# Seven block products of V in one row ahead of both output projections, with VectorE's turns and reads in another order

## The reference

```python
q = heads(x @ Wq + bq)
k = heads(x @ Wk + bk)
v = heads(x @ Wv + bv)
scores = jnp.einsum('bhqd,bhkd->bhqk', q, k) * scale
scores = jnp.where(mask[:, None] == 0, -jnp.inf, scores)
attn = jax.nn.softmax(scores, axis=-1)
out = jnp.einsum('bhqk,bhkd->bhqd', attn, v)
out = out.transpose(0, 2, 1, 3).reshape(b, s, D_MODEL)
x = _layernorm(x + (out @ Wo + bo), axis=-1)
```

## Time and profile before

| what | before |
|---|---|
| median of three runs | 808.75 us |
| the profiled execution | 808.37 us |
| its span, first to last instruction | 806.6 us |
| TensorE busy | 799.6 us (99%) |
| VectorE busy | 635.5 us (79%) |
| GpSimd busy | 540.2 us (67%) |
| ScalarE busy | 267.5 us (33%) |
| mean granted clock of TensorE | 0.998 |

### The profile page before, as it was taken

One profiled execution on the slowest core, in us unless ns is written; L12 is line 12 of the kernel. 1 busy time (PEld: TensorE's weight loads), 2 busy tenths in 40 slices (PEclk: granted clock), 3 DMA queues, 4 the chain that ended last, 5 costly groups with the idle time before them and its releaser, 6 DMA issues.

```text
span 806.6 us, 26965 instructions
## 1 busy us (share of the span) xinstructions
PE 799.6 (99%) x11777; PEld 680.2 (84%) x11777; DVE 635.5 (79%) x1008; ACT 267.5 (33%) x349; POOL 540.2 (67%) x437
## 2 busy tenths in 40 slices
PE   9999999999999999999999999999999999999997
PEld 7888888888888888888888888888888888888876
DVE  5869777878778887778887787877878777876895
ACT  6642333322333222333223332223332333323223
POOL 0387668766678676776766767666866768755672
PEclk9999999999999999999999999999999999999999
DMA  9335435254453434534345344544525435234342
GB/s 330 127 81 173 116 113 179 84 150 130 120 177 98 147 109 119 176 114 134 117 115 171 123 132 119 156 130 119 164 81 171 125 106 178 71 108 120 94 110 103
DMA packets 65110, 106.64 MB, mean 132 GB/s; under 512 B 11744, under 2 KB 28640, under 8 KB 62944
## 3 DMA queue, kind: packets, MB, share of 16 engines
q1 hardware_dynamic: 52512, 87.85, 34.9%
q10 hardware_dynamic: 12480, 17.06, 8.2%
HBM read 54.53 MB, written 16.78 MB: 88 GB/s over the span
## 4 chain that ended last, share of the span: by engine, by line
PE 99%; DMA 0%; DVE 0%; issue 0%; POOLq 0%; POOL 0%
PE ring L373 16%; PE ring L374 15%; PE ring L375 15%; PE ring L525 7%; PE ring L526 7%; PE ring L529 7%; PE psum_s L476 6%; PE psum_s L446 6%; PE ring L467 6%; PE psum_s L480 6%; PE psum_s L478 6%; DMA x_raw<-in_xt 0%; PE ring L393 0%; PE ring L401 0%; PE ring L397 0%
## 5 line engine op out<-in xcount | busy, mean ns | idle before, releaser
L1186 POOL TENSOR_TENSOR soft<-soft,top 128x1024 f32<-128x1024 f32 x62 | 122.6, 1977 | 21.2 <-DVE top L973 21.2
L237 POOL TENSOR_TENSOR soft<-soft,inverse 128x1024 f32<-128x1024 f32 x62 | 118.8, 1917 | 26.0 <-DVE inverse L980 25.9
L977 DVE TENSOR_REDUCE total<-soft 128x16 f32<-128x1024 f32 x62 | 75.3, 1214 | 54.2 <-ACT soft L719 54.2
L719 ACT ACTIVATE soft<-soft 128x1024 f32<-128x1024 f32 x62 | 65.9, 1062 | 112.5 <-POOL soft L1186 112.5
L373 PE MATMUL ring<-x_hi,wk_hi 128*128 128x512 f32 x256 | 102.8, 401 | 0.0
L374 PE MATMUL ring<-x_lo,wk_hi 128*128 128x512 f32 x256 | 99.9, 390 | 0.0
L375 PE MATMUL ring<-x_hi,wk_lo 128*128 128x512 f32 x256 | 99.8, 390 | 0.0
L525 PE MATMUL ring<-wo_hi,ot_hi 128*128 128x512 f32 x252 | 99.2, 394 | 0.0
L526 PE MATMUL ring<-wo_lo,ot_hi 128*128 128x512 f32 x252 | 98.9, 393 | 0.0
L754 ACT CAST s_hi<-v 128x1024 fp32r<-128x1024 f32 x27 | 28.3, 1046 | 207.7 <-DVE v L909 207.7
L373 PE MATMUL ring<-x_hi,wq_hi 128*128 128x512 f32 x248 | 96.7, 390 | 0.0
(11 more groups left out here) (127 smaller groups left out, 1862.0 us busy)
## 6 DMA issues: line engine op xcount, KB each, us to landing
pt<-soft SPq DMA_DIRECT2D x248, 64.0 KB, 2.4
x_raw<-in_xt SPq DMA_DIRECT2D x15, 1024.0 KB, 6.8
row<-in_x SPq DMA_DIRECT2D x60, 256.0 KB, 2.7
out_rows<-row SPq DMA_DIRECT2D x60, 256.0 KB, 2.6
pt<-soft ACTq DMA_DIRECT2D x232, 64.0 KB, 2.4
v<-in_xt SPq DMA_DIRECT2D x27, 512.0 KB, 4.5
adj<-in_adj SPq DMA_DIRECT2D x16, 128.0 KB, 2.7
kt<-in_wk SPq DMA_DIRECT2D x4, 256.0 KB, 6.0
```

What stands on the lines that cost most here:

```text
L237: ops.tensor_tensor(soft_of(c), soft_of(c), on_keys(inverse[:, c % 2, :]), ALU.mult).then_inc(normed, 1)
L977: nc.vector.tensor_reduce(total[:, c % 2, :], by_row_head(soft_of(c)), AX_XY, ALU.add).then_inc(summed, 1)
L1186: nc.gpsimd.tensor_tensor(soft_of(c), soft_of(c), on_keys(top[:, c % 2, :]), ALU.subtract).then_inc(centred, 1)
```

## The change

On TensorE all seven products stand in a row, P3 ahead of P7, and both output projections behind them; the wait for `ot_lo_done` is now behind the seventh product. The product P3 waits for the read of P5, as the third read, which is written out as `READ_5 = 3`. On VectorE `turn(b)` stands straight behind `turn(a)`, ahead of the read of P1; P5 is read before P4; `split_ot` comes behind the read of P6; the two last reads (P3 first, then P7) come ahead of the add of the projection.

```diff
-P1, P2, P4, P5, P6, P7, P3, PARTS = 1, 2, 3, 4, 5, 6, 7, 7
+P1, P2, P4, P5, P6, P3, P7, PARTS = 1, 2, 3, 4, 5, 6, 7, 7
+
+READ_5 = 3
...
             def last_products(m):
+                pe.wait_ge(v_read, v_reads(m) + READ_5)
+                product(other_sums(), *inputs_sum(4), *weights_block(1, 1), adds=True)
                 pe.wait_ge(v_read, v_reads(m) + P6)
                 product(first_sums(), *inputs_sum(3), *weights_sum(3), adds=True)
-                product(other_sums(), *inputs_sum(4), *weights_block(1, 1), adds=True)
...
                 first_products(p)
+                last_products(p)
                 pe.wait_ge(ot_lo_done, p)
                 project_out(a - 2)
-                last_products(p)
                 project_out(b - 2)
...
-                dve.wait_ge(v_part, v_reads(m) + P4)
-                nc.vector.tensor_tensor(quarter(m, 1, 0), second(1), bias_of(0), ALU.add).then_inc(v_read, 1)
                 dve.wait_ge(v_part, v_reads(m) + P5)
                 nc.vector.tensor_tensor(quarter(m, 1, 1), other_sums(), bias_of(1), ALU.add).then_inc(v_read, 1)
+                nc.vector.tensor_tensor(quarter(m, 1, 0), second(1), bias_of(0), ALU.add).then_inc(v_read, 1)
...
+                dve.wait_ge(v_part, v_reads(m) + P3)
+                dve.wait_ge(v_read, v_reads(m) + P6)
+                nc.vector.tensor_tensor(quarter(m, 0, 1), other_sums(), quarter(m, 0, 1), ALU.add).then_inc(v_read, 1)
                 dve.wait_ge(v_part, v_reads(m) + P7)
-                dve.wait_ge(v_read, v_reads(m) + P6)
                 nc.vector.tensor_tensor(both, first_sums().unsqueeze(1).to_broadcast([P, 2, HALF]), both,
                                         ALU.add).then_inc(v_read, 1)
-                dve.wait_ge(v_part, v_reads(m) + P3)
-                nc.vector.tensor_tensor(quarter(m, 0, 1), other_sums(), quarter(m, 0, 1), ALU.add).then_inc(v_read, 1)
...
+                turn(b)
                 if p >= 1:
                     read_first(p)
+                    read_middle(p)
                     split_ot(p - 1)
-                turn(b)
-                if p >= 1:
-                    read_middle(p)
+                    read_last(p)
+                    add_y(a - 2)
+                    row_sums(a - 2)
                 else:
                     read_v(b)
-                if p >= 1:
-                    add_y(a - 2)
-                    read_last(p)
-                    row_sums(a - 2)
```

## The result

The changed kernel takes **830.95 us** (median of five runs, 829.09 to 832.6) against 808.95 us of the kernel before in the same comparison (808.1 to 809.65). The ratio is 1.027, with a 95% interval of 1.0257 to 1.0283: slower by 22 us. Its profiled execution took 831.51 us, of which the span is 829.6.

The account below looks back on a forecast made before the run. TensorE, busy 799.6 of 806.6 us, was taken to bound the kernel. A net 0.62 us a pass plus 0.30 for late passes gave 26 x 0.92 + 2.44 = 26.4 us on 808.37: 835 us, range 820 to 846.

Parts of the forecast that it names:

- forecast A: Main case: the first projection waits for VectorE's later split, also held by late normalisations; 835 us, 828 to 842, chance 0.62.
- The chain: VectorE's masks come 0.40 us later, so normalisation, turn, read 1, product 6, its read, split and projection follow; wait costs 0.68.
- B: Rival: the 0.40 is absorbed, product 6 is not held, only the split's place costs, 0.49 us a pass; 823 us, chance 0.16.
- The restart: TensorE, waiting for VectorE, starts its first matmul 0.14 us behind the end of VectorE's instruction.
- The fresh start: On TensorE after a wait, the first projection pays 0.10 us more; products take 0.70 to their last matmul instead of 0.60.
- The saved switches: On TensorE, fewer switches between products and projections save some 0.03 us each, 0.06 us a pass.
- D: Rival: not slower; the split is ready when TensorE comes and only switches count, 0.8 us saved; 807.6 us, chance 0.04.
- The late passes: GpSimd's waits for the row's load make tile b's normalisation late in some passes; 0.30 us a pass on average.
- C: Rival: row loads land 0.65 us late in all passes, each costing 1.27 us; 844 us, chance 0.14.
- The first pass: Outlier: its normalisation ends 3.12 us behind its first product, so the change costs 2.44 us there.
- What would show it: Signs: gap of 0.5 to 1.3 us before each first projection, smaller one before product 6, period about 25.7 us.
- VectorE's hand-over: VectorE's next instruction starts before the last one ends; otherwise turn to read and read to split each take 0.08 us longer.

Follow-up runs that it names:

- e1: TensorE's row of seven products with both projections behind it, put alone into the kernel before, VectorE's order unchanged: 858.31 us, ratio 1.0614.
- e3: The changed kernel with the turn of tile b moved behind the split of the mixed heads: 820.28 us, ratio 1.014.
- the last experiment: Changed kernel with own banks for projections, bias add behind both normalisations, products ordered 1, 2, 5, 6, 4, 3, 7, turn of b between reads 1 and 2: 809.65 us.

## Why the prediction was right, and where its steps were off

The forecast was 835 us, between 820 and 846, slower with a chance of 0.93; 830.95 came out, by forecast A's mechanism and inside A's own 828 to 842. That an early pass came out within 0.04 us is in part luck: two of its terms were off by more than that, in opposite directions.

| step, us behind the first product unless said | predicted | measured in the pass of 419.05 |
|---|---|---|
| mask behind the scores | 2.86 | 2.86 |
| tile b normalised | 1.30 | 1.30 |
| read of product 1 starts | 2.45 | 2.51 |
| product 6, last matmul | 3.71 | 3.64 |
| read of product 6 starts | 4.03 | 4.00 |
| split done | 5.57 | 5.55 |
| first matmul of the projection | 5.71 | 5.60 |
| early pass longer by | 0.62 | 0.58 |

**The chain** came out link by link: the masks later by 0.40, the normalisation and the turn with them, and then read, product, read, split, projection. The rival that the 0.40 would be absorbed (B) fell on that: it is not absorbed. But what it costs an early pass is only 0.13, by the run with the bias behind; the place of the split is 0.41 (25.20 there to 24.79 once the projections no longer wait), and the waits for reads the last 0.05 (24.79 to 24.74). In the prediction those shares stood much the same, 0.13 for the held product 6 (0.62 less 0.49) and 0.49 for the split.

**The restart** was mis-sized. The prediction took 0.14 us from VectorE's end to TensorE's first matmul, out of a row at the kernel's start. Here it is 0.05 (424.60 to 424.65), and 0.05 again where product 6 is held in the late pass (its read ends at 294.09 + 0.39, its first matmul starts at 294.53) and in e1 (411.15 to 411.20) and e3 (417.96 to 418.01). The fresh start was right: the projection's first matmul takes 0.34 to the next instead of 0.23, 0.11 more.

**The saved switches** were mis-sized the other way, and this covered the first error: 0.06 us a pass in the sum, 0.01 by the last experiment. There the first projection still takes 2.75 (412.08 to 414.83), what it took behind products before, and not 2.72; only the second is shorter, 2.81 against 2.84. Some 0.02 of that is lost between scores and products, for a cause that I have not found. So D, a row in which only switches count, was not to be had in this kernel, and its saving of 0.8 us did not come even where no steady pass waits. The Trainium skill ("Perfetto Trace Analysis", section "Matmul Optimizations") wants matmuls back to back in batches since the engine's power follows its use. Here the clock was already in its top tenth, and the longest row without a wait bought nothing that can be measured.

**The late passes** cost 25.57 - 25.33 = 0.24 on the mean, where I took 0.30. They are others than before, but not more of them: tile b is normalised over 0.1 us later than in the early passes in 13 of the 26 passes of the trace of before and in 12 of the changed kernel's, on the mean of all 26 by 0.30 and 0.25 us. The list of waits is longer (19.3 us in 18 waits, where the earlier trace rows had 11.3 in 14), but by waits for tile b's own row, the longest of 3.4 among them, and those stand behind the normalisation. The waits for tile a's row in these passes come to 5.9 us in nine, where they were 6.3 in ten. The pass of 276.53 is a late one, with 1.12 us of GpSimd's wait and 0.81 of TensorE's. The mechanism is shown by the run that moved the bias away from it; which passes will be late was not to be had from the trace of before. C, all passes late, did not come.

**The first pass** cost 2.13 where I had 2.44. The normalisation ends 62.46 - 59.48 = 2.98 behind the first product, not 3.12. And the prediction had the first pass wrong in one point: it took TensorE not to be held there before the change. On the timeline of the kernel before, the first projection of that pass is

```profile
63.11 0.50 PE L525 MATMUL ring<-wo_hi,ot_hi 128*128 128x512 f32 x1
```

which is 3.72 behind the first product instead of 3.70, and its next matmul starts 0.33 later instead of 0.23. It waited for a split that stood behind a late turn of tile a and ended at 61.85 + 1.21 = 63.06. So 0.12 of the cost was there already: 0.58 + 2.98 - 1.30 - 0.12 is 2.14.

**The tail** behind the last pass is shorter by 0.6 us, which no step of the prediction has. Of this 0.4 is one pause inside the mix, at 772.86 in the trace of the kernel before, with no releaser; the trace of e3 has such a pause too (0.5 at 784.97), so it does not come from the old order. Its cause and the other 0.2 stay open. The four differences, 26 x 0.04 for the early passes, 26 x 0.06 for the late ones, 0.3 and 0.6, make 3.5 us; the sum of 834.8 was 3.3 above the profiled execution.

**What would show it** was read as told: the gap ahead of the first projection is there in each pass, but as 0.25 us past the usual pitch (424.28 + 0.12 to 424.65) and not as 0.5 to 1.3. The rest of what the split costs hides in products 6 and 3, which wait themselves (422.02 and 422.86) and run under the split. The period grew to 25.57, not 25.7. The gap ahead of product 6 is there in ten passes, 1.5 us in the first; ahead of product 3 there is a small one, which this list left out; the working had named it, under the split, and there it lies. It is larger than the working had it: read 2 adds to what read 1 wrote and waits for it, so it starts 0.49 behind it (421.56 to 422.05) and not 0.33, and read 5, which product 3 needs, comes later by the difference.

**VectorE's hand-over** went by the row: the turn ends at 420.39 + 1.25 = 421.64, and the read behind it starts at 421.56, before that end. The Trainium skill ("VectorE: DVE Perf Modes", section "The DRAIN you can't avoid") says that the next op waits for an empty pipe, except where it is not held; by its main rule the sum would have been 839, and the row agrees with the exception. Of the 8 us between 839 and what came, 4 are this rule's, and the rest are the other terms above.

## What to carry over

When an order on the bounding engine is changed, follow the reads on the other engine that its instructions need, with start and end of each, from the event that both share; the lead in the old order (here 1.1 us) is what decides. Such a change on two engines is one decision (TensorE's row alone cost 49 us, with VectorE's new order 22), so price it as a whole. And put what may come late (a load that hangs on a store) behind the work that the bound engine waits for, even where the order before had room for it: here the load follows such a store (in the chain that ended last one store takes 3.64 us from 200.44, and the load starts at 204.09), and that one move was worth 9 us of the 22, some 6 of them in the late passes.

## What the runs showed of the hardware

Two things show in several places. A TensorE that waits for VectorE starts its first matmul only 0.05 us behind the end of VectorE's instruction (four places in three kernels), yet that first matmul then takes longer to the next: 0.34 instead of 0.23 us with 512 columns, 0.22 instead of 0.12 with 256. And a wait too short to be listed still shows in that pitch: product 6 starts on time in the early pass (422.02) and has its second matmul 0.20 later. Such losses, 0.1 us at a time, are in no list of waits here; they were found only from start to start.
